# Perceiver kernel on one core: the head of the quantised self-attention written as one block

## The reference, cut to what matters

```python
def _L1_attn_ref(x, ln_gamma, ln_beta, w_qkv, w_out, log_temp):   # x is _layernorm(stream)
    ...
    mu = jnp.mean(x, axis=-1, keepdims=True)
    var = jnp.var(x, axis=-1, keepdims=True)
    h = (x - mu) * jax.lax.rsqrt(var + LN_EPS)                    # the second norm
    h = h * fq_round(ln_gamma) + fq_round(ln_beta)
    qkv = fq_floor(fq_floor(h) @ fq_round(w_qkv))
    q, k, v = jnp.split(qkv, 3, axis=-1)                          # 16 heads of 64
    ...
    temp = jnp.exp(log_temp[0])
    temp = temp + jax.lax.stop_gradient(jnp.floor(temp * 4096.0) / 4096.0 - temp)
    dots = jnp.einsum('bhnd,bhmd->bhnm', q, k) * temp
    dots = fq_floor(dots)
    ...                                                           # softmax, fq_floor, @ v, fq_floor, @ fq_round(w_out)
```

## Time and profile before

| | us |
|---|---|
| median of 3 runs (lowest, highest) | 2666.25 (2664.68, 2667.53) |
| the profiled execution | 2666.86 |
| its span in the profile | 2665.0 |
| busy in the span: PE, DVE, ACT, POOL | 2229.0, 1711.6, 1442.8, 458.0 |

### The profile page before, as it was taken

One profiled execution on the slowest core, in us unless ns is written; L12 is line 12 of the kernel. 1 busy time (PEld: TensorE's weight loads), 2 busy tenths in 40 slices (PEclk: granted clock), 3 DMA queues, 4 the chain that ended last, 5 costly groups with the idle time before them and its releaser, 6 DMA issues. The chain is left out here.

```text
span 2665.0 us, 80517 instructions
## 1 busy us (share of the span) xinstructions
PE 2229.0 (84%) x26087; PEld 1655.4 (62%) x26087; DVE 1711.6 (64%) x5620; ACT 1442.8 (54%) x3658; POOL 458.0 (17%) x1104
## 2 busy tenths in 40 slices
PE   5999999988759997999999999995357117499998
PEld 3777777767636665888888888884125103344444
DVE  4888888877654443777777777776789878701100
ACT  5888888876612223544554454453578747632221
POOL 2444444433213230000000000000000030000000
PEclk9999999999869997999999999998698555799999
DMA  3222222210100003444444444442000000100001
GB/s 92 75 73 73 73 73 73 73 38 1 26 0 0 0 0 92 113 109 106 113 109 104 106 116 104 108 110 71 0 0 0 0 1 4 45 0 0 0 0 32
DMA packets 257634, 140.91 MB, mean 53 GB/s; under 512 B 40176, under 2 KB 255616, under 8 KB 257152
## 3 DMA queue, kind: packets, MB, share of 16 engines
q1 hardware_dynamic: 257536, 139.61, 19.9%
HBM read 118.57 MB, written 20.97 MB: 52 GB/s over the span
## 5 line engine op out<-in xcount | busy, mean ns | idle before, releaser
L1075 DVE CUSTOM_DVE_ANT_0 c_SM<-c_bs,c_MB 128x257 f32<-128x257 f32 x512 | 211.1, 420 | 125.9 <-PE c_bs L979 124.2
L1052 ACT ACTIVATE c_OT<-c_bo 128x512 f32<-128x512 f32 x128 | 76.4, 597 | 389.5 <-PE c_bo L992 389.5
L979 PE MATMUL c_bs<-c_cT,c_QP 128*128 128x257 f32 x1024 | 264.1, 396 | 9.9 <-DVE c_LT L1094 9.9
L992 PE MATMUL c_bo<-c_PT,c_C 32*128 32x128 f32 x8192 | 266.0, 277 | 2.5 <-DVE c_PT L1090 2.3
L677 ACT ACTIVATE a_PR<-a_SM,a_nmx 128x257 f32<-128x257 f32 x512 | 253.4, 499 | 4.0 <-issue 3.3
L1046 ACT ACTIVATE c_PR<-c_SM,c_nmx 128x257 f32<-128x257 f32 x512 | 253.3, 504 | 0.0
L992 PEld LDWEIGHTS c_bo<-c_PT,c_C 32*128 32x128 f32 x8192 | 241.6, 187 | 18.6 <-issue 4.0
L979 PEld LDWEIGHTS c_bs<-c_cT,c_QP 128*128 128x128 f32 x1024 | 182.2, 190 | 56.6 <-issue 24.0
L724 DVE CUSTOM_DVE_ANT_0 a_SM<-a_bs,a_MB 128x257 f32<-128x257 f32 x512 | 187.9, 422 | 44.5 <-PE a_bs L545 38.6
L1090 DVE STREAM_TRANSPOSE c_PT<-c_PR 128x256 f32<-128x256 f32 x512 | 181.2, 411 | 0.0
L949 POOL TENSOR_TENSOR c_XL<-quarter,c_PR 128x16 f32<-128x16 f32 x128 | 27.6, 216 | 738.8 <-DVE c_PR L1085 738.8
(11 more groups left out here) (489 smaller groups left out, 4901.3 us busy)
## 6 DMA issues: line engine op xcount, KB each, us to landing
c_C<-in_ctx_dram SPq DMA_DIRECT2D x512, 128.0 KB, 2.8
a_C<-in_ctx_dram SPq DMA_DIRECT2D x128, 128.0 KB, 2.1
ctxT_dram<-a_cT SPq DMA_DIRECT2D x128, 128.0 KB, 1.9
c_cT<-ctxT_dram SPq DMA_DIRECT2D x128, 128.0 KB, 2.5
a_MK<-in_mask_Bx1xSxS_bk_dram SPq DMA_DIRECT2D x128, 32.1 KB, 1.9
X<-in_x_dram SPq DMA_DIRECT2D x4, 512.0 KB, 6.2
g_h<-in_L_ffn_h_w_dram SPq DMA_DIRECT2D x2, 1024.0 KB, 8.5
out_dram<-X SPq DMA_DIRECT2D x1, 2048.0 KB, 8.7
```

The lines of the kernel that those rows point to most:

```text
L979: nc.tensor.matmul(b_s[hg][:, 0:SK], QP[:, r // 4 % 2, r % 4, 4 * hg:4 * hg + 4, :], cT[:, r, :], start=True, stop=True).then_inc(s_ps, 1)
L992: last = nc.tensor.matmul(b_o[:, h, 0:P], C[rows, buf, kb, :], PT[rows, s.r % 2, kb, :, :], start=(kb == 0), stop=(kb == NKB - 1), tile_po ...
L1075: nc.vector.tensor_tensor_reduce(SM[:, par, hg, :], b_s[hg][:, 0:SK], MB[:, :], 1.0, NEG1, ALU.add, ALU.max, mx[:, par, hg:hg + 1]).then_i ...
```

## The change

The head becomes one block, and the call of `phase_norm` goes away.

- Both norms are folded into one chain on the statistics of `X`. The variance of the first norm's output is v / (v + eps), so the second norm's result is (x - m) / sqrt(v (1 + eps) + eps^2). There is one set of the 13 small instructions; `d_n_inner` and its 32 `bn_stats` are gone.
- Each group of four tiles is normed half by DVE and half by ACT into `d_xn`, which has four buffers (`XB`), as has the PSUM tile `d_tp`. ACT's copy out of PSUM applies gamma and beta (`weighted`), so the two passes over `d_XNT` are gone.
- The maximum of h is taken for each group (`largest`, 128x512) and not for each half.
- POOL makes three reductions (gamma and beta; the weights; h), and the 54 resets stand behind them.
- The weights' maxima stand between the groups' norms on DVE. log_temp is loaded last.
- exp(log_temp) and the product with `u_dot` move to the start of DVE's program in the dots' block, ahead of its wait for `k0_ok`.

```diff
-            phase_norm(nc, sh, "d_n_", loads, rounds=2)
             block = ctx.enter_context(nc.Block())
...
             @block.gpsimd
             def _(pool):
-                pool.wait_ge(maxed, 1)
-                pool.partition_all_reduce(ma[:, 0:4], mm[:, 0:4], P, REDUCE.absmax).then_inc(all_max, 1)
-                pool.wait_ge(maxed2, 1)
-                pool.partition_all_reduce(ma[:, 4:6], mm[:, 4:6], P, REDUCE.absmax).then_inc(all_max, 1)
+                for i, cols in enumerate((slice(0, 2), slice(2, 4), slice(4, 5))):
+                    pool.wait_ge(maxed, i + 1)
+                    pool.partition_all_reduce(ma[:, cols], mm[:, cols], P, REDUCE.absmax).then_inc(all_max, 1)
+                clear_retired(pool)
+
+            @block.tensor
+            def _(pe):
+                for g in range(NG):
+                    pe.wait_ge(xnv_ok, g + 1)
+                    pe.wait_ge(xna_ok, g + 1)
+                    wait(pe, h_ok, g - XB + 1)
+                    for t in range(4):
+                        last = nc.tensor.transpose(tp[g % XB][:, t * P:(t + 1) * P], xn[:, g % XB, t, :], sh.ident[:, :])
+                    last.then_inc(turned, 1)
...
-                    part = sh.XNT[:, i * HALF:(i + 1) * HALF]
-                    nc.scalar.activation(part, part, ACT.Identity, bias=g_q[:, 1:2], scale=g_q[:, 0:1]).then_inc(h_ok, 1)
...
+                def weighted(g):
+                    act.wait_ge(turned, g + 1)
+                    nc.scalar.activation(columns(g), tp[g % XB][:, :], ACT.Identity, bias=g_q[:, 1:2],
+                                         scale=g_q[:, 0:1]).then_inc(h_ok, 1)
...
+                normalised(0)
+                normalised(1)
+                act.wait_ge(gq_ok, 1)
+                for g in range(NG):
+                    weighted(g)
+                    if g + 2 < NG:
+                        normalised(g + 2)
+                act.wait_ge(ws_ok, 1)
...
+                nc.vector.tensor_scalar(var, var, 1.0 + LN_EPS, LN_EPS * LN_EPS, ALU.mult, ALU.add).then_inc(var_ok, 1)
...
+                dve.wait_ge(gb_in, 32)
+                absmax(mm[:, 0:2], g_f[:, :].unsqueeze(2)).then_inc(maxed, 1)
+                normalised(0)
+                normalised(1)
                 dve.wait_ge(all_max, 1)
-                pot_scale(nc, link, ma[:, 0:4], y4[:, :], p4[:, :], s4[:, :], i4[:, :])
+                pot_scale(nc, link, ma[:, 0:2], y4[:, 0:2], p4[:, 0:2], s4[:, 0:2], i4[:, 0:2])
...
+                normalised(2)
+                normalised(3)
+                dve.wait_ge(wq_in, 16)
+                link(absmax(mm[:, 2:3], wq_f[:, :]))
+                dve.wait_ge(wo_in, 16)
+                absmax(mm[:, 3:4], wo_f[:, :, :].rearrange("p a d -> p (a d)")).then_inc(maxed, 1)
+                normalised(4)
+                normalised(5)
+                largest(0)
                 dve.wait_ge(all_max, 2)
-                link(nc.vector.tensor_tensor(ma[:, 4:5], ma[:, 4:5], ma[:, 5:6], ALU.max))
+                pot_scale(nc, link, ma[:, 2:4], y4[:, 2:4], p4[:, 2:4], s4[:, 2:4], i4[:, 2:4])
+                dve.sem_inc(ws_ok, 1)
+                normalised(6)
+                largest(1)
+                normalised(7)
+                for g in range(2, NG):
+                    largest(g)
+                nc.vector.tensor_reduce(mm[:, 4:5], mh[:, :], AX.X, ALU.max).then_inc(maxed, 1)
+                dve.wait_ge(lt_in, 16)
+                dve.wait_ge(all_max, 3)
                 pot_scale(nc, link, ma[:, 4:5], y4[:, 0:1], p4[:, 0:1], c("s_h"), c("i_h"))
...
                 link(nc.vector.tensor_tensor(c("u_dot"), c("s_qkv"), c("s_qkv"), ALU.mult))
-                link(nc.vector.tensor_tensor(c("u_dot"), c("u_dot"), c("temp"), ALU.mult))
...
                 def _(dve):
+                    link = chain_of(dve, chain)
+                    n_, r_, e_ = (tmp[:, i:i + 1] for i in range(3))
+                    link(nc.vector.tensor_scalar(ni[:, 0:1], lt[:, :], 1.4426950408889634, None, ALU.mult))
...
+                    link(nc.vector.tensor_scalar(c("temp"), ni[:, 0:1], 1.0 / 4096, None, ALU.mult))
+                    link(nc.vector.tensor_tensor(c("u_dot"), c("u_dot"), c("temp"), ALU.mult))
                     dve.wait_ge(k0_ok, 1)
```

More of the change, by code:

```diff
@@ L1661, in phase_attn1 @@
[L1661 to L1662 removed]
+            tp = [psum(f"d_tp{i}") for i in range(XB)]
+            gb_in, lt_in, wq_in, wo_in = sem("d_gb_in"), sem("d_lt_in"), sem("d_wq_in"), sem("d_wo_in")
+            chain, var_ok, std, norm_ok = sem("d_chain"), sem("d_var_ok"), sem("d_std"), sem("d_norm_ok")
+            maxed, all_max = sem("d_maxed"), sem("d_all_max")
+            xnv_ok, xna_ok, turned, h_ok = sem("d_xnv_ok"), sem("d_xna_ok"), sem("d_turned"), sem("d_h_ok")
@@ new lines, in phase_attn1, with _ @@
+            gq_ok, ws_ok, sh_ok = sem("d_gq_ok"), sem("d_ws_ok"), sem("d_sh_ok")
+            wq8_ok, wo8_ok, q8_ok = sem("d_wq8_ok"), sem("d_wo8_ok"), sem("d_hq8_ok")
+            HALF = T // 2
+            total, mean, diff, dsq, m2, var, rstd, half, shift = (small[:, i, :] for i in range(9))
+            columns = lambda g: sh.XNT[:, 512 * g:512 * (g + 1)]
+            block = ctx.enter_context(nc.Block())
+            @block.sync
+            def _(sp):
+                sp.dma_start(g_f[:, 0:1], gamma.rearrange("(d a) -> d a", a=1)).then_inc(gb_in, 16)
+                sp.dma_start(g_f[:, 1:2], beta.rearrange("(d a) -> d a", a=1)).then_inc(gb_in, 16)
+                sp.dma_start(wq_f[:, :], w_qkv).then_inc(wq_in, 16)
+                sp.dma_start(wo_f[:, :, :], w_out.rearrange("(a p) d -> p a d", p=P)).then_inc(wo_in, 16)
+                sp.dma_start(lt[:, :], bcast(log_temp, 0, P)).then_inc(lt_in, 16)
```

105 lines of the change are left out of this document (62 added, 43 removed).

## The result

| | before | after |
|---|---|---|
| median of the runs, us | 2666.89 (2664.68 to 2668.34, 4 runs) | 2634.42 (2631.84 to 2636.39, 4 runs) |
| ratio, 95% interval | | 0.9878 [0.9861, 0.9895] |
| profiled execution, us | 2666.86, span 2665.0 | 2631.84, span 2629.8 |
| first DVE instruction of the head | 1841.78 | 1842.47 |
| busy PE / DVE / ACT / POOL, us | 2229.0 / 1711.6 / 1442.8 / 458.0 | 2214.0 / 1691.9 / 1439.0 / 458.8 |

The change took 32.5 us off the median; 33.2 were forecast. The four runs lie in two pairs, 2631.8 and 2632.7, then 2636.1 and 2636.4. Their median falls between the pairs, where no run is, and by the interval of the ratio the totals alone put the gain only between 28 and 37 us.

The account below looks back on a forecast made before the run. The head was taken as a chain carried by DVE, the next two blocks as DVE's too. Head -34.7 us and dots +1.5 make -33.2, from a median of 2666.25 to 2633.0; range 2630.5 to 2637.5.

Parts of the forecast that it names:

- 1: chain on the statistics ends: Head's start on DVE: `floor_bias` at 0.1 us, then the chain on the statistics, 3.36, ending at 1845.24.
- 4: maximum of `w_qkv` begins: Head, on DVE: maxima of `w_qkv` 3.4 us and `w_out` 1.25, then norms of groups 4 and 5, 1.2; until 1856.95.
- 6: `pot_scale` begins: Head's end: POOL's third reduction, 0.5 us, then the unchanged tail from `pot_scale` to the matmul, 6.85; until 1872.55.
- Step 2: Head: POOL's first reduction begins 6.0 us behind its configuration, a new DVE wait of 1.6; restart at 1848.2.
- The norm instruction: Head, on DVE: each norm instruction 0.30 us, 1.2 for two groups; possibly 0.28 to 0.35 without the loop.
- The check of the other engines: Head: PE, ACT and POOL stay hidden behind DVE; ACT 1.4 us a group, 0.8 to spare on h, POOL 1.5.
- step 5: Head, on DVE: weights' scales 1.0 us, groups 6 and 7 with a maximum 1.93, six maxima 4.4, final maximum 0.2.
- The resets: Head's end: POOL's 54 resets, 4.1 us, run from 1865.7 to 1869.9, hidden with 1.5 to spare.
- The moved chain: Dots' block start: 28 links, 5.26 us, 3.7 hidden by POOL's memset of `d_K` and 1.5 exposed.
- The rival of the shared port: Dots' block: the chain's first instruction waits until POOL's memset is over, 3.5 us on top, 2636.5; 12%.
- the slower rival: Two blocks behind the head: TensorE's clock stays at 1.2 GHz, at the full 78 us 2711; 2%.
- the rivals' arithmetic: Head's groups: ACT or PE sets the pace, from 1.8 us a group; at 2.1 about 3 us, 2636; 8%.

Follow-up runs that it names:

- experiment 1: The changed kernel with GpSimd configured ahead of the head, by a memset and an all-reduce on unused columns; 2633.01 us, ratio 0.9869.
- experiment 3: The changed kernel with GpSimd configured ahead of the head and exp(log_temp) on GpSimd in the QKV block; 2629.46 us, ratio 0.9856.
- Experiment 7: The changed kernel with one reduction of four columns for gamma, beta and both weights instead of two; 2637.47 us, ratio 0.9892.
- experiment 8: The changed kernel with GpSimd's 54 semaphore resets ahead of its first reduction instead of behind the third; 2641.38 us, ratio 0.9907.
- Experiment 2: The changed kernel with exp(log_temp) on GpSimd in the QKV block instead of on DVE in the dots' block; 2634.09 us, ratio 0.9877.

## Why the prediction came out

Counted from the head's first DVE instruction, forecast and measured:

| step | forecast | measured |
|---|---|---|
| 1: chain on the statistics ends | 3.46 | 3.45 |
| 2: DVE restarts behind the first reduction | 6.42 | 6.94 |
| 4: maximum of `w_qkv` begins | 9.32 | 9.55 |
| 5: the six maxima begin | 18.8 | 18.67 |
| 5: maximum over eight begins | 23.2 | 22.99 |
| 6: `pot_scale` begins | 23.9 | 23.75 |
| 6: QKV's first weight load | 30.8 | 30.63 |

The path is the one that was forecast, and the sum held to 0.2 us at each of the last four marks. That the medians came within 0.7 of the forecast is in part luck: they can't tell so closely, two errors of some half a microsecond in the steps cancel (the next two points), and two stretches that no step had moved by +1.06 and -3.9 in the profiled execution.

- **Step 2, the new wait, was mis-sized.** The mechanism held, as experiment 1 shows, but the gap was 6.6 instead of 6.0, inside the range of 5.8 to 7.1, and the wait 2.40 instead of 1.6; 0.3 of the difference is that DVE came earlier. The Trainium skill (GPSIMD Engine Reference, "Instruction dispatch") has about 6 us for the first call of freshly loaded code; here it was 5.7 and 5.8 where POOL was configured in the block before (experiments 1 and 3), 6.6 in the head, and 7.5 behind the resets.
- **The norm instruction** was taken at 0.30, the loop's. Without the loop four took 1.10 and started 0.25 apart. It gives back 0.2 for each pair of groups, and with that the 0.5 of step 2 is gone by step 5.
- **The check of the other engines held in its result.** I had taken an evacuation at 0.60, the plain copy's; with gamma and beta it took 0.77, and two norms 0.87. A group started every 1.43 us, as the 1.4 said. ACT's quantisation of the weights ended at 1867.15, in the same hundredth as DVE's instruction that makes the scale of h, so there was no time to spare at that joint; its half of h ended at 1869.33, 1.5 before DVE's last cast of h, where I had 0.8. Experiment 7 shows what happens when ACT starts 5.7 later: +2.9.
- **The resets** lay behind the third reduction and ended at 1869.8, 2.1 before DVE's last instruction of the block. Put first they cost 4.96 (experiment 8), more than their own 4.1.
- **The moved chain:** +1.5 forecast, which had the small block's -0.19 in it; measured +1.80 in the dots' block and -0.24 in the small one, +1.56. Experiment 2 had 1.73 of the 1.80 back. The rival of the shared port fell: the chain's first link started 0.04 behind the memset and not at its end, its 28 links took 5.3 us, as the 28 before did with no memset near, and the memset took 3.51 in both. A rule on the same page as the one that I weighed then (the Trainium skill, SBUF — State Buffer, "Who interferes with whom") agrees: an instruction with two inputs in SBUF contends with a GpSimd instruction that reads SBUF and not with one that only writes, as a memset does. No run here puts a wide cast beside the memset.
- **The clock behind the head** was granted at 0.85 (before 0.86), so the slower rival fell too.
- **One slip in the rivals' arithmetic** changes no step: at 2.1 us a group ACT would end at 1866.7, 2.4 behind the 1864.3 at which DVE wants it, and not 3.
- **What no step of it had:** +1.06 in the residual stretch, from a loop that the change does not touch, and the feed-forward stretch, 347.8 to 352.3 whatever the kernel. Head, small block and dots together are -33.3, against -33.2 forecast. With both of them, the start's +0.7 and the middle's +0.3 the sum is the profiled -35.2. How they fell in the runs without a trace, and so in the medians' -32.5, is not known; the first alone would give -32.3.

What each part is worth, each undone or done alone: the exact chain instead of two rounds 23.4 (from the side of before), gamma and beta at the evacuation 4.4, their own reduction ahead of the weights' maxima 2.9, exp out of the head 2.6 net. The last three are from the side of after and overlap, so they don't sum to the remaining 11.5.

The fastest kernel is that of experiment 3, 2629.46, and with the loop written out 2629.38, which the runs can't tell from it. What bounds their head is DVE's chain, with three waits left: 0.3 for ACT's square root, 0.2 for `w_qkv` and 0.6 for the third reduction.
